# Causal attention's end: two queues for the last head's transfers, the residual added by TensorE, statistics read from PSUM

## What is computed

```python
qkv = x @ Wqkv + bqkv                        # x is layernorm(stream)
q, k, v = split, 16 heads of width 8
att = softmax(where(causal, q @ k.T / sqrt(8), -inf))
y = (att @ v).transpose(0, 2, 1, 3).reshape(b, t, c)
stream = stream + (y @ Wproj + bproj)
```

## Time and profile before

| | us |
|---|---|
| three runs | 968.80, 967.94, 971.24 |
| their median | 968.8 |
| the profiled execution's own time | 966.31 |
| its span | 964.6 |
| mean granted clock of TensorE | 0.918 |

### The profile page before, as it was taken

One profiled execution on the slowest core, in us unless ns is written; L12 is line 12 of the kernel. 1 busy time (PEld: TensorE's weight loads), 2 busy tenths in 40 slices (PEclk: granted clock), 3 DMA queues, 4 the chain that ended last, 5 costly groups with the idle time before them and its releaser, 6 DMA issues. The chain is left out here.

```text
span 964.6 us, 16498 instructions
## 1 busy us (share of the span) xinstructions
PE 747.5 (77%) x6011; PEld 498.1 (52%) x6011; DVE 708.9 (73%) x1214; ACT 359.0 (37%) x602; POOL 396.8 (41%) x586
## 2 busy tenths in 40 slices
PE   0466797777769999857687893579899999878893
PEld 0245445766669998535554562334444444354462
DVE  8999688899996879799943235599899999065232
ACT  1122382110004631112131351428788888622251
POOL 3344302888887940134506254033333333204253
PEclk9989799999998999888879996759999999998997
DMA  7100000000000000310001312655200000000313
GB/s 186 29 1 0 2 1 1 1 1 1 1 1 1 2 2 0 115 33 1 0 1 46 84 39 76 218 93 109 38 10 9 10 9 10 11 1 31 85 39 112
DMA packets 41236, 33.94 MB, mean 35 GB/s; under 512 B 6438, under 2 KB 35686, under 8 KB 41158
## 3 DMA queue, kind: packets, MB, share of 16 engines
q1 hardware_dynamic: 38022, 26.80, 11.5%
q0 software_dynamic: 2560, 5.31, 1.7%
q10 hardware_dynamic: 576, 0.79, 0.3%
HBM read 17.51 MB, written 13.80 MB: 32 GB/s over the span
## 5 line engine op out<-in xcount | busy, mean ns | idle before, releaser
L2041 DVE TENSOR_REDUCE blockmax<-c_bank 128x8 f32<-128x1024 f32 x144 | 173.2, 1219 | 22.4 <-PE c_bank L2174 18.3
L2110 ACT ACTIVATE PT<-c_bank 128x1024 f32<-128x1024 f32 x144 | 146.8, 1026 | 37.4 <-PE c_bank L2196 35.1
L2210 PE MATMUL c_bank<-PT,V 128*9 128x256 f32 (+1 forms) x1408 | 86.7, 343 | 3.7 <-ACT OT L2102 2.6
L915 PE MATMUL sums<-prod,ident 128*128 128x128 f32 x512 | 67.8, 289 | 26.7 <-DVE prod L947 26.7
L2167 PE MATMUL c_bank<-KA,QA 48*128 48x128 bf16 (+3 forms) x608 | 60.6, 284 | 23.9 <-DMA QA<-qk_parts_dram 11.8
L915 PEld LDWEIGHTS sums<-prod,ident 128*128 128x128 f32 x512 | 62.5, 200 | 31.9 <-DVE prod L947 31.8
L1991 POOL TENSOR_SCALAR_AFFINE_SELECT PT<-PT 128x256 f32<-128x256 f32 x128 | 49.1, 407 | 69.5 <-ACT PT L2110 69.3
L1676 POOL DMA_INDIRECT routed_results<-results_m,rows_m x48 | 45.9, 957 | 64.2 <-DVE results_m L1650 62.4
L1656 DVE TENSOR_TENSOR r_h_m<-r_silu_m,r_gu_m 128x256 f32<-128x256 f32 x48 | 20.2, 421 | 66.0 <-ACT r_silu_m L1641 66.0
L391 PE MATMUL gu_f<-gu_wT,xqT_f 128*128 128x352 f32 x128 | 51.0, 551 | 17.8 <-DVE h_f L311 17.8
L1390 POOL DMA_INDIRECT sorted_rows<-xs_m,where_m x32 | 30.9, 967 | 77.7 <-DVE where_m L1514 68.6
(11 more groups left out here) (342 smaller groups left out, 1790.1 us busy)
## 6 DMA issues: line engine op xcount, KB each, us to landing
sorted_rows<-blank SPq DMA_DIRECT2D x2, 1584.0 KB, 12.3
rows_m<-sorted_rows SPq DMA_DIRECT2D x12, 264.0 KB, 5.0
back_m<-routed_results SPq DMA_DIRECT2D x8, 256.0 KB, 3.7
qk_parts_dram<-qk_parts SPq DMA_DIRECT2D x8, 256.0 KB, 2.6
qk_parts_dram<-qk_parts SPq DMA_DIRECT2D x4, 384.0 KB, 2.8
QA<-qk_parts_dram SPq DMA_DIRECT2D x6, 256.0 KB, 4.6
KA<-qk_parts_dram SPq DMA_DIRECT2D x6, 256.0 KB, 7.2
m_gu<-in_rt_gate SPq DMA_DIRECT2D x1, 1024.0 KB, 6.1
```

The costliest lines, as they stand in the source:

```text
L915: ins = nc.tensor.matmul(sums[:, kind, 0], k.ident[:, :], prod[:, kind, e // HALF, :, e % HALF, :], start=(e == 0), stop=(e == DH - 1))
L2041: nc.vector.tensor_reduce(blockmax[:, h % 2, :, HALFQ * n:HALFQ * (n + 1)], slot_of((1, m)).rearrange("p b (n c) -> p b n c", c=P), AX.X, ...
L2110: nc.scalar.activation(PT[:, u % PRING, :, :], slot_of((0, u)), ACT.Exp, scale=SCALE).then_inc(s_pt, 1)
L2210: ins = nc.tensor.matmul(O[32 * g:32 * g + DH + 1, f * P:f * P + n], V[:, b, j, h, :], PT[:, u % PRING, b, o:o + n], start=(a % len(VALUES ...
```

## The change

The last head's groups 1 and 3 are issued by ScalarE, groups 0 and 2 by SyncE. TensorE waits for the last OT copy and the bias sum, multiplies the unit matrix with the residual (128 x 512, f32, four times) into banks 4 to 7, runs three fillers into bank 0 in place of nine, and projects onto what lies in the banks (start=False). VectorE's adds go; its statistics read the banks, and ScalarE copies each bank back to `k.x` behind them.

```diff
+        def output_of(eng, h, g):
+            par, b = divmod(g, BATCH)
+            dst = YT[h * DH:(h + 1) * DH, b, :].rearrange("p (n two c) -> p two n c", two=2, c=P)[:, par]
+            eng.dma_start(dst, OT[32 * g:32 * g + DH, h % 2, :].rearrange("p (n c) -> p n c", c=P)).then_inc(s_yt[h % 2], 16)
+            eng.dma_start(den[h * DH + 2 * g:h * DH + 2 * g + 2, :], OT[32 * g + DH:32 * g + DH + 1, h % 2, :]).then_inc(s_yt[h % 2], 16)
...
             @block.sync
                 def send_out(h, groups):
                     sp.wait_ge(s_ot, h + 1)
                     for g in groups:
-                        par, b = divmod(g, BATCH)
-                        dst = YT[...]
-                        sp.dma_start(dst, OT[...]).then_inc(s_yt[h % 2], 16)
-                        sp.dma_start(den[...], OT[...]).then_inc(s_yt[h % 2], 16)
+                        if h < HEADS - 1 or g % BATCH == 0:
+                            output_of(sp, h, g)
...
             @block.vector
-                dve.wait_ge(s_bias, 1)
                 for g in range(4):
                     dve.wait_ge(s_y, g + 1)
-                    xr = k.x[:, 4 * g:4 * g + 4, :].rearrange("p t c -> p (t c)")
-                    nc.vector.tensor_tensor(xr, xr, bank[:, 4 + g, :], ALU.add).then_inc(s_sum, 1)
-                    dve.wait_ge(s_sum, g + 1)
-                    k.tile_stats(4 * g, 4)
+                    for t in range(4 * g, 4 * g + 4):
+                        ins = nc.vector.bn_stats(k.stats[:, t, :], bank[:, 4 + g, (t % 4) * D:(t % 4 + 1) * D])
+                    ins.then_inc(s_sum, 1)
...
             @block.scalar
+                act.wait_ge(s_ot, HEADS)
+                for g in range(1, 2 * BATCH, BATCH):
+                    output_of(act, HEADS - 1, g)
+                for g in range(4):
+                    act.wait_ge(s_sum, g + 1)
+                    nc.scalar.copy(k.x[:, 4 * g:4 * g + 4, :].rearrange("p t c -> p (t c)"), bank[:, 4 + g, :])
...
             @block.tensor
-                keep_busy(k, bank[:, 4, :], 9)
+                pe.wait_ge(s_ot, HEADS)
+                pe.wait_ge(s_bias, 1)
+                for g in range(4):
+                    nc.tensor.matmul(bank[:, 4 + g, :], k.ident[:, :], k.x[:, 4 * g:4 * g + 4, :].rearrange("p t c -> p (t c)"),
+                                     start=True, stop=False, skip_group_check=True)
+                keep_busy(k, bank[:, 0, :], 3)
                 pe.wait_ge(s_rec, 1)
...
-                pe.wait_ge(s_ot, HEADS)
                 for t in range(TILES):
...
                     ins = nc.tensor.matmul(bank[:, 4 + t // 4, (t % 4) * D:(t % 4 + 1) * D], YT[:, t // QT, o:o + P],
-                                           wp[:, :], start=True, stop=True)
+                                           wp[:, :], start=False, stop=True, skip_group_check=True)
```

## The result

| | before | after |
|---|---|---|
| median of 20 runs, us | 971.12 | 966.04 |
| lowest to highest | 966.67 to 974.18 | 960.90 to 969.86 |
| profiled execution, its span | 966.31, 964.6 | 969.86, 968.1 |

The ratio on record is 0.9953 (95% interval 0.9934 to 0.9971). Of 971.12 that is 4.6 us faster, with an interval from 2.8 to 6.4; the two medians lie 5.1 apart. The profiled execution after is the slowest of its twenty and longer than the one before; it has to be read by stretches, that is, by positions counted from one instruction to another inside the part that the edit touches.

A forecast was written before the change was run, and what follows sets the result against it. At the end of causal attention, SyncE's transfer issuing (5.74 us) and VectorE's tail (3.50) were taken to bind. Gains of 2.59 and 1.99, in all 4.6, took the median from 968.8 to 964.2; range 961.5 to 966.4.

The forecast's parts named there:

- The absolute time: Whole kernel: median going from 968.8 us, over three runs, to 964.2, range 961.5 to 966.4.
- the sum: End of causal attention: 2.59 us before the selector matmuls plus 1.99 in the tail, 4.6 gained.
- Part 1 and 2: Last head's transfers from two queues and TensorE's new order: selector matmuls start at 843.69 in place of 846.28, 2.59 us gained.
- The bounds: Last head's transfer issuing: 2.88 us gained if ScalarE issues like SyncE, 0 if the queues take turns.
- What I named as late next: Before the selector matmuls: TensorE's fourteen passes, 6.0 us, end 0.15 after the reciprocal and set the start.
- Part 3: Tail behind the projection: adds gone, statistics from PSUM paced by TensorE every 0.86 us, 1.99 gained.
- Accumulating projection, bias wait, residual by the unit matrix: TensorE's new work at the end of causal attention: each priced at no extra cost.
- The clock: TensorE at the next stage: fall after 2.6 us idle somewhat likelier; rival that it holds, 962.5, chance 0.24.
- My price of 1.7: Next stage's fillers: a fallen clock delays the transposes behind them by 1.7 us.
- statistics pacing the tail: Rival, tail: VectorE's statistics from PSUM set the pace, gain there 1.2 to 1.0 us, 965.0 to 965.2; chance 0.12.
- Two queues not side by side: Rival, last head's transfers: reciprocal starts where it did, only the tail's 2.0 us gained, 966.8; chance 0.09.
- Slower: Rival: TensorE's new wait for OT drops the clock to half through this stage, 8.7 us slower, 977.5; chance 0.03.

The follow-up runs named there:

- queues_only: Changed kernel with nine fillers, adds and statistics from SBUF kept, only the last head's transfers over two queues; selectors 7.70 us after the OT copy's start, 1.6 gained.
- warm: Changed kernel with ScalarE also issuing one transfer of head 14 while waiting for the last value matmuls; reciprocal 0.45 us sooner, selectors at 6.83.
- after_again: Changed kernel, unedited, run again beside the kernel before on another chip; stretch from OT copy to next stage 17.16 us, ratio 0.9940.
- scalar_alone: Changed kernel with all eight transfers of the last head issued by ScalarE; first transfer 1.35 us, selector matmuls 5.41 in place of 3.72.
- tail_only: Changed kernel with all eight transfers back on SyncE and five fillers in place of three; 1.96 us gained, all behind the projection.
- balanced: Changed kernel with one transfer moved to SyncE, so SyncE issues five and ScalarE three; reciprocal 0.1 us sooner.
- before_fill: Kernel before with three fillers of 512 columns added behind the projection; transposes 3.51 us after the next stage's start, ratio 0.9973.
- after_fill: Changed kernel with one filler of 512 and one of 256 columns added behind the projection; first scatter 1.86 us sooner, ratio 0.9938.
- best: Changed kernel with ScalarE's early head 14 transfer, two fillers before the selectors, and 512- and 256-column fillers behind the projection; ratio to the kernel before 0.9920.
- best_again: The same kernel as best, run again beside the changed kernel on another chip; ratio to the kernel before 0.9935.

## Why the prediction was right or wrong

- **The absolute time** missed. Twenty runs of the kernel before have a median of 971.12, 2.3 over the three that I had; 0.9953 of it is 966.6, just over the upper end of my range (966.4), though the median of the changed kernel's runs, 966.04, is just under it. The step that failed is the base of the sum: I set the gain against 968.8 from three runs and allowed some 1.3 for scatter, where it measured 971.12 and single runs of one kernel lie 7.5 to 9.0 apart. The spread belonged into the range.
- **The ratio** came out at 964.2 / 968.8 = 0.9953 to the last digit, and that is luck. The stretch that the sum describes gave 3.97 and not 4.6, the measured gain has an interval from 2.8 to 6.4, another chip gave 0.9940, and what makes up the difference was not forecast.
- **Part 1 and 2, sized at 2.59, measured 2.00** (the same in both profiles of the changed kernel). It is the term of the gain that was mis-sized. ScalarE's issue was priced at 5% over SyncE's from side-by-side transfers of another shape, where no first issue was dear; here the first cost 1.57 for 0.72. The bounds held it. With it the reciprocal's end (7.22), not TensorE's fourteen passes, decides: TensorE stood idle for 0.37 before the selectors. What I named as late next was late only in `queues_only`, with its eighteen passes; in `warm` the fourteen passes (through at about 6.75) and the reciprocal's end (6.77) were level.
- **Part 3, sized at 1.99, measured 1.96.** The mechanism was right, TensorE paced it. Its pace was misread, though: the first adds started 0.11 after their bank was ready, so 0.86 is too short. The 32 passes of the projection start (3.73 - 0.27) / 31 = 0.112 apart, so eight take 0.89. ScalarE's copies were 0.89 apart, and the last four statistics started 860.57 - 860.53 = 0.04 behind the projection's end, no later than the first four behind theirs. A statistic from PSUM took 0.284 us on the mean, from SBUF 0.281; four took 0.89 for 0.87, a start every 0.204 for 0.199. Of the 0.065 for each instruction, an estimate from the table of the Trainium skill ("VectorE: DVE Perf Modes", section on the TRN2 errata), this trace shows under 0.01; the measurement decides.
- **Accumulating projection, bias wait, residual by the unit matrix:** 7.28 for 7.29, and eight residual passes in 3.54, 0.1 more than at the fillers' pace, all of it in the first pass and hidden behind the reciprocal; so nothing, as priced.
- **The clock:** I took the fall as likelier. Behind a gap of about 2.6 it fell in four profiled executions (`after`, `after_again`, `warm`, `scalar_alone`) and held in two (`tail_only`, `balanced`); behind 4.55 it fell in both, behind 1.3 to 2.0 it held in all four. So it goes either way, as the chances said. My price of 1.7 was right for the fillers and wrong for the program. Up to the scatter the held cases gained anything from 0 to 2 us, since the clock falls once more under the router matmuls; between the gap of 4.55 (19.64, two executions) and that of 2.6 (18.55, six) it is 1.1 on the mean. To the end of the program the profiles show no gain from a clock held at the fillers (the table below). Only the ratio of `before_fill`, 0.9973 and barely clear of 1, speaks for one. What the change gains beyond 3.97 stays open.
- **Rivals:** statistics pacing the tail: false. Two queues not side by side: false. Slower: its mechanism exists, behind a wait of 2.94; the wait of 0.70 that the change adds for OT caused no fall in any profile.

From the next stage's start to the last instruction, in us, kernels of one chip in one row:

| clock fell at the fillers | clock held at the fillers |
|---|---|
| `before` 106.5, `after` 105.0 | none |
| `queues_only` 112.7 | `tail_only` 112.9, `after_fill` 112.1, `balanced` 110.7 |
| `warm` 105.4, `scalar_alone` 106.1 | `before_fill` 106.2, `best` 105.6 |
| `after_again` 110.9 | `best_again` 110.8 |

## What to carry to other kernels

Where a chain waits for eight small transfers from one queue, as here, their issue time is what it waits for. A second queue took 2.0 of 5.7 us off it, and 2.45 where its own first issue was already behind it: give it one transfer in an idle moment before. When a chain gets shorter, count the fillers that were sized for the longer one. An edit worth half a per cent is read from positions inside its stretch; single executions differ by more in code that nobody touched.

## What the runs showed of the hardware

- ScalarE's first transfer of this end took 1.32 to 1.57 us of its queue in nine profiled executions of nine, the following ones of the same two shapes 0.61 to 0.78. The cause is open: ScalarE had issued none for some 210 us, but the first it ever issued, at 621 us, took at most 0.45.
- With both queues' last transfers issued 0.15 apart, the reciprocal, which waits for all of them, started 2.07 after the start of the last issue (`warm`), against 1.76 with SyncE's queue alone.
- In eleven of the twelve profiled executions the clock fell 7.7 to 11.6 after the next stage's start, under its router matmuls or just behind them, with no idle time of TensorE over 0.33 since that start. Where it had held at the fillers, that fall came sooner, at 7.7 to 9.3 for 10.0 to 11.6. The exception is `after_fill`: it first fell at 17.3, while TensorE was idle for 3.8.
